# Mamba's unit loop on TensorE: the sum over the state moved ahead of the slot's preparation job

## The reference

```python
x = silu(conv(x_in)); delta = softplus(x @ wd1.T @ wd2.T + wd2_b)
Bm = x @ wB.T; Cm = x @ wC.T
h = exp(delta[:, None] * A) * h + (delta * x)[:, None] * B[None, :]   # per token
y = sum over n of h[:, n] * C[n]
y = (y + x * W_D) * silu(skip)
out = resid + y @ out_w.T
```

## Time and profile before

| | |
|---|---|
| median of 3 runs | 2038.39 us (2036.72 to 2038.93) |
| time of the profiled execution | 2038.59 us |
| its span in the trace | 2036.9 us |
| Mamba's loop in it | about 58 to 942 us |
| VectorE in that loop | 831.63 of 884 us busy |
| TensorE in that loop | 759.96 of 884 us busy |

### The profile page before, as it was taken

How to read it: one execution, slowest core, us unless ns; L and a number is a source line. 1 busy time by engine, 2 the same in 40 slices (tenths; PEclk the granted TensorE clock), 3 DMA queues, 4 the chain that set the end, 5 groups by cost and what they waited for, 6 DMA issues and landing times. The chain is left out here.

```text
span 2036.9 us, 27560 instructions
## 1 busy us (share of the span) xinstructions
PE 1812.9 (89%) x9655; PEld 1418.8 (70%) x9655; DVE 1478.3 (73%) x2279; ACT 1054.1 (52%) x1773; POOL 1035.7 (51%) x612
## 2 busy tenths in 40 slices
PE   6888889888989898666799999997999699999999
PEld 2555565656565565455488888886777578888888
DVE  4899999999999999996766666663343555555555
ACT  6775767677776767342444444432333253333333
POOL 2888898989898988874311111111444511111111
PEclk9899999999999999777899999998999899999999
DMA  6222232333323232322000000000000000000000
GB/s 188 76 81 99 85 95 92 90 92 93 93 88 94 91 96 85 93 85 90 0 1 0 0 0 0 0 0 27 1 0 0 0 1 11 10 10 10 10 10 21
DMA packets 55619, 97.78 MB, mean 48 GB/s; under 512 B 10736, under 2 KB 10864, under 8 KB 54896
## 3 DMA queue, kind: packets, MB, share of 16 engines
q1 hardware_dynamic: 55536, 96.74, 15.1%
HBM read 92.00 MB, written 4.72 MB: 47 GB/s over the span
## 5 line engine op out<-in xcount | busy, mean ns | idle before, releaser
L329 POOL TENSOR_TENSOR m_U<-m_U,m_C 128x1024 f32<-128x1024 f32 x256 | 603.5, 2366 | 69.3 <-DVE m_U L751 58.9
L628 ACT ACTIVATE m_dA<-m_delta,m_negA 128x512 f32<-128x512 f32 x512 | 344.4, 685 | 177.0 <-DVE m_U L751 175.1
L456 PEld LDWEIGHTS m_y<-m_ident,m_U 128*128 128x128 f32 x2048 | 258.7, 151 | 114.5 <-issue 72.9
L751 DVE TENSOR_TENSOR_SCAN m_U<-m_dA,m_carry,m_U 128x512 f32<-128x512 f32 x256 | 312.2, 1267 | 7.0 <-ACT m_dA L628 6.6
L456 PE MATMUL m_y<-m_ident,m_U 128*128 128x128 f32 x2048 | 291.9, 290 | 25.5 <-POOL m_U L329 25.4
L751 DVE TENSOR_TENSOR_SCAN m_U<-m_dA,m_U 128x512 f32<-128x512 f32 x256 | 296.9, 1207 | 16.6 <-ACT m_dA L628 13.1
L734 DVE TENSOR_TENSOR m_U<-m_dx,m_psB 128x1024 f32<-128x1024 f32 x208 | 249.3, 1199 | 27.8 <-PE m_psB L440 27.7
L440 PE MATMUL m_psB<-m_stack,m_pick 128*128 128x512 f32 x208 | 110.8, 533 | 66.8 <-DVE m_U L734 66.4
L1100 POOL TENSOR_TENSOR gl_S<-gl_Rt 128x1024 f32<-128x1024 f32 x16 | 31.6, 1997 | 271.5 <-ACT gl_Rt L1208 271.5
L1100 POOL TENSOR_TENSOR fl_S<-fl_Rt 128x1024 f32<-128x1024 f32 x16 | 31.6, 1997 | 264.9 <-ACT fl_Rt L1208 264.9
L1428 POOL TENSOR_TENSOR a_rinv<-a_ssq,a_mhalf 128x64 f32<-128x64 f32 x8 | 84.3, 10550 | 113.5 <-DVE a_ssq L1643 113.5
(11 more groups left out here) (319 smaller groups left out, 4438.0 us busy)
## 6 DMA issues: line engine op xcount, KB each, us to landing
m_C<-bc_rows SPq DMA_DIRECT2D x256, 256.0 KB, 3.1
m_B<-bc_rows SPq DMA_DIRECT2D x48, 256.0 KB, 3.5
fq_whole<-in_ffn_w SPq DMA_DIRECT2D x4, 1024.0 KB, 8.1
out<-res SPq DMA_DIRECT2D x8, 512.0 KB, 2.8
res<-in_x SPq DMA_DIRECT2D x1, 3072.0 KB, 12.6
res<-in_x SPq DMA_DIRECT2D x2, 512.0 KB, 4.6
a_whole<-in_Wkvqu SPq DMA_DIRECT2D x1, 1024.0 KB, 4.8
m_inw<-in_in_w SPq DMA_DIRECT2D x1, 512.0 KB, 4.6
```

Of the source, the lines that this page charges most:

```text
L329: pool.tensor_tensor(u, u, C[:, M % C_RING, :].unsqueeze(1).to_broadcast([P, PE_E, CHUNK]), ALU.mult).then_inc(hc_ready, 1)
L456: last = nc.tensor.matmul(y[:, t, j * P:(j + 1) * P], U[:, M % U_RING, j, t * P:(t + 1) * P], ident[:, :], start=False, stop=n == N - 1, i ...
L628: nc.scalar.activation(dA[:, s % A_RING, :], delta[:, q, e, :], ACT.Exp, scale=negA[:, e, n:n + 1]).then_inc(dA_ready, 1)
L751: nc.vector.tensor_tensor_scan(u, dA[:, s % A_RING, :], u, carry[:, e, n:n + 1] if q else 0.0, ALU.mult, ALU.add).then_inc(scan_done, 1)
```

## The change

In TensorE's loop the slot's jobs are issued after `nsum(M - 2)` instead of before it.

```diff
             for M in range(ALL_UNITS):
                 if M + 2 < ALL_UNITS and M + 2 not in pool_units:
                     spread_B(M + 2)
-                for name, k in parts_of(PE_AT, M):
-                    part(name, k)
                 if M == 2:
                     pe.wait_ge(taps_ready, KE + 1)
                     for b in (2, 3):
                         pe.wait_ge(free[b], HEAD_TAKEN[b])
                 if M >= 2:
                     nsum(M - 2)
+                for name, k in parts_of(PE_AT, M):
+                    part(name, k)
             nsum(ALL_UNITS - 2)
             nsum(ALL_UNITS - 1)
```

## The result

The changed kernel takes 2094.07 us (median of 4 runs, 2091.89 to 2096.44) against 2038.15 us of before (4 runs): a ratio of 1.0275, 95% interval 1.0258 to 1.0293, 56 us slower. The direction and the mechanism were as forecast, and the time lies in the range; the forecast of 2083 us was 11 us short.

The account below looks back on a forecast made before the run. The prediction took VectorE's work and its waits to bound the loop. Terms of 22.2 + 5.5 + 2.4 - 0.5 + 15.3 = 44.9 us on 2038 gave 2083 us, range 2058 to 2108 at about 0.8.

Parts of the forecast that it names:

- Where the bound lies: In the loop over the units: VectorE is busy 831.63 of 884 us, so the loop lasts its work plus 52 us standing.
- The job behind a gate: At 13 gates: the half job now stands between sum and spread, delaying VectorE's mult by 1.71 us each, 22.2 us.
- The chain through `bl+`: Behind gate0: ScalarE's copy behind `bl+` and the decay after it come 0.79 us later in 7 chunks, 5.5 us.
- The rest of the slots: Outside the gates: only slot 30 pays, 0.6 us in 4 chunks, 2.4 us; GpSimd's other late products are taken up.
- The clock: Behind the gates: TensorE's longer standing brings a low-clock stretch costing 1.7 us at 9 of 13 gates, 15.3 us.
- 2.06 did not: At gate1: TensorE standing 2.06 us did not lower its clock, so standing 2.8 to 3.8 us need not either.
- rival B: At the gates: clock low throughout each, or GpSimd's lateness not taken up; 85 us, 2123, or 2108 by half; chance 0.12.
- rival C: In VectorE's later waits: they swallow the delay, no change, 2038, or 2063 if 17.9 us of decay waits shrink; chance 0.04.
- The rule's extreme: At all 13 gates: by the skill's rule alone each runs at the low level, 4.27 us each, 55.5 us, the upper bound.
- The first chunk: In slot 2: TensorE can start the skip term without waiting for in0's copy, a gain of up to 0.7, taken as 0.5 us.
- A: At the gates: the clock stays up, leaving 29.6 us, 2068 us, or 2062 if ScalarE's 5.5 is hidden; chance 0.28.
- D: At VectorE's mults: the 26.9 us of waits are really for ring `U`, so an earlier sum removes them; 2012 us; chance 0.03.

## Why the prediction was right, and where it was short

**Where the bound lies: right.** VectorE's work changed by 0.1 us, and the loss is time in which VectorE waits.

**The job behind a gate: right.** 13 x 1.71 = 22.2 us was forecast. The extra matmuls behind the gate cost 23.6 us, and at a gate crossed at the high level the wait is 2.60 us, against 0.88 before.

**The chain through `bl+`: right in its sum.** 5.5 us was forecast; the sum in slot 19 alone cost 6.1. In the changed kernel it shows in two pieces, 0.28 and 0.71 us at the gate0 of chunk 1: the copy of bc, which I had called just hidden, is not hidden quite. The kernel with three extra matmuls has the same two waits, so they are not the clock's. Over the seven chunks the waits for decays behind gate0 grew by 6.4 us. All waits for decays were forecast at 24 us and came to 27.0; 2.7 of them stand where VectorE had waited for GpSimd.

**The rest of the slots: right.** I gave 2.4 us to slot 30. Everything outside the gate slots cost 7.7 us, and 6.1 of it is slot 19; what stays for all others is 1.6 us, less than the measurement's uncertainty. The trace shows the term itself: VectorE's waits for the spread at the end of chunks 0, 2, 4 and 6 were 0.53, 0.54, none and 0.54 us and are 1.11, 0.82, 0.80 and 1.23, together 2.35 us more. GpSimd's late products ahead of that are taken up as forecast.

**The clock: right in kind, too small.** The step of the prediction that was short is "I take that at 9 of the 13 gates: 15.3 us". The trace has it at 13 of 13, 12 of them new. Take from the 61.4 us of waits the 14.0 of before and the 22.2 of the half jobs: 25.2 us stay for the clock. Against a crossing at the high level (2.60 to 2.72 us) it took 1.6 to 1.7 us at 8 gates, the price that I gave to one, and 2.5 to 3.0 at 5 gates, since there the low level lasted through the skip term and the sum and at most of them reached the half job. That is 9.9 us of the 11 that the forecast was short; the misses of the other terms nearly cancel. The experiment that keeps TensorE at work ahead of the gate shows that this is the clock: with three extra matmuls all 13 low crossings are gone, the 13 waits fall from 61.4 to 34.6 us with the same instructions on the path, and the time by 26 us (+55.9 to +29.5).

The premise "2.06 did not" was weak. It was read from one gate; at gate0 of chunk 0 the same trace had a low stretch behind 1.91 us of standing, and two gates of the kernel with only slot 19 changed had one behind 2.06. A smaller slip: by their own terms rival B's 2108 is 2107 and rival C's 2063 is 2065 (2083 - 17.9); nothing rests on either.

The Trainium skill, "TensorE: Matmul & The Clock Gate", Part 1, has the low level as the default that activity lifts. The measurement agrees in the main, at gates as at the pause of the earlier trace rows. Over the gates of all 12 profiled kernels, where TensorE stood 2.4 to 3.9 us ahead of the gate, part of the way behind it was at 1.2 GHz in 38 of 39 crossings (the one exception is the 3.88 us shown above); where it stood 1.9 to 2.3 us, in 13 of 39; where it stood 1.8 us or less, in none of 82 (the start of the loop is not counted). So the pause alone does not decide. The rule's extreme, 4.27 us at each gate, did not come: the mean was 1.9.

**The first chunk.** I took 0.5 us as the gain from the skip term that need not wait for in0's copy. VectorE's first wait there fell from 4.26 to 1.78 us, but in the kernel with the job last in gate slot 2 alone, whose program is the same up to that point, it was 3.88: there the skip term took 3.75 us at the low level, and 2.02 in the changed kernel. Two kernels that keep the old order up to there (slot 18 alone, slot 19 alone) have 1.97 and 1.96. So most of the 2.5 us is the clock at the start, which differs from run to run; at the high level the gain is 0.2 us.

**The rivals.** A, the clock stays up, did not come by itself; made by experiment, it gives 29.5 us. B did not come either. C is out: the waits for decays did not shrink but grew. D is out: the waits for the spread grew, and at no gate does the trace show a mult waiting for the ring.

**What stays open.** Whether a low crossing of one gate makes that of the next likelier: the two kinds of gate alone sum to 43.7 us and together to 49.0. The runs at hand do not settle it. Nor do they say what decides between the two levels behind pauses of the same length, as behind 2.15 us in the kernel with two extra matmuls: low at two gates, high at one.

## What to carry to other kernels

Where an engine has to wait for another one and that one then waits for it in turn, the order around the wait has a price on one side only: work ahead of the wait is free as long as it fits into it, work behind it is paid in full, 1.7 us for 1.7 us, and 13 times over here. Before moving work away from a wait "to get the important thing done first", look at which instruction ends that wait; here the sum could not start any earlier, and the cover was lost for nothing.

Better than either order is to take the blocking instruction off the path: the sum that waits for the gate was needed by nobody soon, and the spread behind it was. Moving it behind the spread gave 23 us.

On TensorE the lost cover is paid twice, since a longer pause ahead of a path mostly brings a lower clock on the path. Matmuls that compute nothing, put into such a pause, bought back 26 of 56 us.

## What the runs showed that I had not expected

Extra matmuls made a kernel faster: 39 of them, in the 13 pauses, took it from 2094 to 2066 us, though they are 35.6 us more of work for TensorE:

```profile
L352 PE MATMUL m_job<-m_taps,m_ident 128*128 128x512 f32 x78 | 35.6, 592 | 0.0
```

This is their group in the kernel with three in each pause.

The length of TensorE's pause did not fix the clock behind it. A pause of 1.91 us was followed by a low stretch in five profiled kernels, all at gate0 of chunk 0, and in five other crossings, one of them at that same gate, it was not. In the kernel with only the gate slots changed one of 3.88 us was not either, while every other pause of 2.4 us and more was. One profile with a clean crossing behind 2.06 us is no proof that 2.06 us are safe.

A pair of ScalarE's table loads more in each chunk (2 x 1.28 us) went with a kernel 10.4 us faster (2013.51 to 2003.10 us), because one wait of 2.1 to 2.3 us in each chunk became two of 0.3 to 0.5 us, and the waits for the spread fell by 3.1 us.
